# Attention row maxima from the scores' own operands, with a separate small stack of scaled keys

## What is computed

```
h = patches(x) @ W.T + b                                  # 32 images, 256 tokens, 256 wide
n = layernorm(h)
q, k, v = n@wq (16 heads of 16), n@wk, n@wv (4 heads of 16 each); rotary embedding on q and k
scores = q.k / 4, causal;  attn = softmax(scores);  h = h + (attn @ v) @ wo
h = h + ffn(layernorm(h))                                 # fake-quantised gate, up and down weights
```

## Time and profile before

| | us |
|---|---|
| median of 3 runs (826.69 to 829.05) | 828.56 |
| the profiled execution: its time | 829.71 |
| its span, first to last instruction | 828.0 |
| busy: PE / DVE / ACT / POOL | 706.0 / 648.1 / 580.7 / 569.2 |
| PE busy between 90 and 460 us, of 370 | 345.3 |

### The profile page before, as it was taken

The page is one execution under the profiler, slowest core; times in us unless marked ns, Lnnn a source line. Parts: engine busy times, 40 slices in busy tenths (PEclk is TensorE's granted clock), DMA queues, the critical chain, the costliest instruction groups (busy, mean ns, idle before and its releaser), DMA issues. The chain is left out here.

```text
span 828.0 us, 20605 instructions
## 1 busy us (share of the span) xinstructions
PE 706.0 (85%) x6706; PEld 372.8 (45%) x6706; DVE 648.1 (78%) x1048; ACT 580.7 (70%) x908; POOL 569.2 (69%) x561
## 2 busy tenths in 40 slices
PE   3577989898999999999999999999876459997894
PEld 2343545454555455545545555445322223332663
DVE  5955788788878888888888887887654359999894
ACT  3345777777788787778877778877555258886783
POOL 1355778787887888888788888786644148884363
PEclk9699999999999999999999999999868669999798
DMA  8235667666566655566666556654443123221499
GB/s 277 58 77 115 117 122 140 137 121 118 131 143 133 143 142 130 117 137 141 133 150 141 119 124 143 137 137 86 88 74 69 53 38 51 51 43 21 70 175 162
DMA packets 237190, 94.46 MB, mean 114 GB/s; under 512 B 214240, under 2 KB 232416, under 8 KB 237152
## 3 DMA queue, kind: packets, MB, share of 16 engines
q1 hardware_dynamic: 228704, 85.59, 47.7%
q0 software_dynamic: 8448, 8.39, 7.0%
HBM read 24.74 MB, written 16.78 MB: 50 GB/s over the span
## 5 line engine op out<-in xcount | busy, mean ns | idle before, releaser
L1200 DVE TENSOR_REDUCE act_all<-pair 128x4 f16<-128x1024 f32 (+1 forms) x192 | 235.1, 1225 | 30.7 <-PE pair L535 29.9
L826 ACT ACTIVATE ffn<-pair 128x768 f32<-128x768 f32 x128 | 103.2, 806 | 76.7 <-PE pair L552 76.7
L975 POOL TENSOR_SCALAR_AFFINE_SELECT act_all<-act_all 128x512 f32<-128x512 f32 x128 | 104.8, 829 | 68.7 <-ACT act_all L826 68.7
L975 POOL TENSOR_SCALAR_AFFINE_SELECT ffn<-ffn 128x512 f32<-128x512 f32 x128 | 92.8, 726 | 65.6 <-ACT ffn L826 65.6
L482 PE MATMUL pair<-act_all 128*128 128x256 f16 (+1 forms) x960 | 116.8, 275 | 17.7 <-DVE act_all L1247 15.4
L826 ACT ACTIVATE act_all<-pair 128x768 f32<-128x768 f32 x128 | 103.6, 809 | 34.2 <-PE pair L552 34.0
L482 PEld LDWEIGHTS pair<-act_all 128*128 128x128 f16 (+1 forms) x960 | 90.2, 98 | 35.8 <-issue 19.5
L1014 POOL TENSOR_TENSOR act_all<-act_all 128x1280 f16<-128x1280 f32 x31 | 81.3, 2622 | 18.7 <-ACT act_all L781 18.7
L550 PE MATMUL pair<-act_all 64*128 64x256 f16 x512 | 73.4, 283 | 11.5 <-ACT ffn L826 4.3
L496 PE MATMUL pair<-act_all 128*128 128x384 f16 x384 | 76.4, 337 | 0.1
L1186 DVE TENSOR_TENSOR act_all<-act_all 128x512 f16<-128x512 f32 x32 | 27.1, 847 | 58.1 <-ACT act_all L819 58.1
(11 more groups left out here) (133 smaller groups left out, 1492.3 us busy)
## 6 DMA issues: line engine op xcount, KB each, us to landing
act_all<-x_t SPq DMA_DIRECT2D x32, 640.0 KB, 4.2
out<-act_all SPq DMA_DIRECT2D x32, 256.0 KB, 2.6
out<-ffn POOLq DMA_DIRECT2D x16, 512.0 KB, 6.8
act_all<-act_all SPq DMA_TRANSPOSE x192, 2.8
act_all<-w_down SPq DMA_DIRECT2D x1, 704.0 KB, 8.8
act_all<-w_emb SPq DMA_DIRECT2D x1, 640.0 KB, 3.9
ffn<-w_gate SPq DMA_DIRECT2D x1, 640.0 KB, 7.1
ffn<-w_up SPq DMA_DIRECT2D x1, 640.0 KB, 8.0
```

The source lines that it names most:

```text
L826: act.activation(probs[i // 4][:, o:o + 2, 0:3, :].rearrange("p h k s -> p h (k s)"), pair[1][:, :].rearrange("p (h c) -> p h c", h=2)[:, ...
L975: pool.affine_select(out=p, in_=p, pattern=[[0, 4], [1, P]], compare_op=ALU.is_ge, fill=0.0, base=0, channel_multiplier=-1).then_inc(maske ...
L1200: dve.tensor_reduce(to, pair[2][:, :].rearrange("p (k g t) -> p k g t", k=2, g=n_), AX.X, ALU.max).then_inc(unit_reduced, 1)
```

## The change

- `max_stack`, `max_op` and `high` are gone. The queries of the units now come from the stack itself: two DMAs transpose its 16 query heads, one for each half of the tokens, 8 blocks each, into `max_q`.
- The keys of the units come from a new `key_stack` (64 columns a head, scaled by 1/64, only the columns opposite to the queries' high part filled), copied by ScalarE at the start of `fill_stack` and transposed into `max_k` by one DMA of 4 blocks. The block masks move to free columns of the stacks and of `key_stack`.
- SyncE's `turn_max` becomes `turn_max_first` (keys, queries of the first half) and `turn_max_second` (queries of the second half). The first waits for `key_ready`, `stack_filled` and `low_ready` of its image.
- The units' products use 64 rows by 128 columns of TensorE, and so do the triangles, with a wider identity `eye_wide`. Count and width of these matmuls stay the same.

```diff
-MAX_SCALE = 1.0 / 8.0
+MAX_SCALE = 1.0 / 64.0
...
-        max_stack = part(TB * QK * 32, FP16).rearrange("p (b h k) -> p b h k", b=TB, h=QK)
-        max_op = part(5 * TOKENS, FP16).rearrange("p (b g t) -> p b g t", b=TB, g=5)
+        key_stack = part(TB * KV * 64, FP16).rearrange("p (b h k) -> p b h k", b=TB, h=KV)
+        max_q = part(8 * TOKENS, FP16).rearrange("p (b g t) -> p b g t", b=TB, g=8)
+        max_k = [ffn[:, 4608 + 256 * k:4864 + 256 * k].bitcast(FP16).rearrange("p (b g t) -> p b g t", b=TB, g=2)
+                 for k in range(2)]
...
-            def turn_max(n):
-
-                sp.wait_ge(high_ready, n + 1)
+            def turn_queries(n, tb, turned):
+
+                sp.dma_start_transpose(max_q[:, tb], stacks[n % 2][:, tb, 0:HEADS, :].rearrange("p h k -> p (h k)")
+                                       ).then_inc(turned[n % 2], 16)
+
+            def turn_max_first(n):
+
+                sp.wait_ge(key_ready, n + 1)
+                sp.wait_ge(stack_filled, n + 1)
+                sp.wait_ge(low_ready, n + 1)
+                if n > 0:
+                    sp.wait_ge(unit_scored, (n - 1) * PAIRS_U + 2)
+                sp.dma_start_transpose(max_k[n % 2].rearrange("p b g t -> p (b g) t"),
+                                       key_stack.rearrange("p b h k -> p (b h k)")).then_inc(
+                                           max_first_turned[n % 2], 16)
+                turn_queries(n, 0, max_first_turned)
+
+            def turn_max_second(n):
+
                 if n > 0:
                     sp.wait_ge(unit_scored, n * PAIRS_U)
-                sp.dma_start_transpose(max_op.rearrange("p b g t -> p (b g) t"),
-                                       max_stack.rearrange("p b h k -> p (b h k)")).then_inc(max_turned[n % 2], 16)
+                turn_queries(n, 1, max_second_turned)
...
                 if (x + 2).exists():
-                    turn_max(x.n + 2)
+                    turn_max_first(x.n + 2)
+                    turn_max_second(x.n + 2)
                 if (x + 1).exists():
                     turn_stack(x.n + 1)
...
                 if p == 0:
-                    pe.wait_ge(max_turned[y.parity], y.half * 16 + 16)
+                    pe.wait_ge(max_first_turned[y.parity], y.half * 32 + 32)
+                if p == 2:
+                    pe.wait_ge(max_second_turned[y.parity], y.half * 16 + 16)
...
                     for g in range(GROUPS):
-                        for j in range(2):
-                            kv = 2 * p + j
-                            rows = slice(32 * kv, 32 * kv + 32)
-                            pe.matmul(max_bank[j][:, g * P:(g + 1) * P], max_op[rows, 0, g, :],
-                                      max_op[rows, 0, 4, :], start=(g == 0), stop=False, skip_group_check=True)
+                        for rows, b in zip(halves, max_bank):
+                            pe.matmul(b[:, g * P:(g + 1) * P], max_q[rows, 0, 2 * g + p, :], keys[rows, 0, p, :],
+                                      start=(g == 0), stop=False, skip_group_check=True)
...
-                        mm = pe.matmul(on_diagonal, eye_b[t, t],
-                                       tri_b[t, t].rearrange("p (a t) -> p a t", a=1).to_broadcast([64, n_, 64]),
+                        at_ = 64 * ((t + j) % 2)
+                        mm = pe.matmul(on_diagonal, eye_wide[rows, at_:at_ + P],
+                                       tri_b[rows, rows].rearrange("p (a t) -> p a t", a=1).to_broadcast([64, n_, 64]),
...
-            def high(x):
-
-                z = x + 2
-                act.wait_ge(qk_ready, z.n + 1)
-                wait(act, max_turned[z.parity - 1], (z + -1).half * 16 + 16)
-                act.activation(max_stack[:, :, :, 0:16], qk[:, :, :, :], ACT.Copy, scale=MAX_SCALE).then_inc(
-                    high_ready, 1)
-
             def fill_stack(x):
...
+                wait(act, max_first_turned[z.parity - 1], (z + -1).half * 32 + 32)
+                act.activation(key_stack[:, :, :, 16:32], qk[:, :, HEADS:QK, :], ACT.Copy, scale=MAX_SCALE).then_inc(
+                    key_ready, 1)
                 act.activation(stack[:, :, :, 16:32], qk[:, :, :, :], ACT.Copy)
```

More of the change, by code:

```diff
@@ L140, in vit_layer @@
         eye_k = sb("eye_k", [P, P], F32)
-        eye_b = sb("eye_b", [P, P], BF16)
+        eye_wide = sb("eye_wide", [P, P + 64], BF16)
+        eye_b = eye_wide[:, 0:P]
         ffn = sb("ffn", [P, 5120], F32)
@@ L517, in unit_pair @@
                 else:
                     for g in range(2):
[L520 to L525, removed]
@@ L527, in unit_pair @@
-                halves = (slice(0, 64), slice(64, 128)) if p % 2 == 0 else (slice(64, 128), slice(0, 64))
-                for j in range(2):
-                    for t in halves:
+                        for rows, b in zip(halves, max_bank):
+                            pe.matmul(b[:, g * TOKENS:(g + 1) * TOKENS].rearrange("p (b t) -> p b t", b=TB),
+                                      max_q[rows, 1, 2 * (2 * (p // 2 - 1) + g) + p % 2, :], keys[rows, :, p % 2, :],
+                                      start=(g == 0), stop=False, skip_group_check=True)
@@ L530, in unit_pair @@
+                for t in range(2):
+                    for j, rows in enumerate(halves):
+                        block_ = slice(64 * t, 64 * t + 64)
                         if p < 2:
-                            on_diagonal = max_bank[j][t, :].rearrange("p (g t) -> p g t", g=GROUPS)[:, :, t]
+                            on_diagonal = max_bank[j].rearrange("p (g t) -> p g t", g=GROUPS)[:, :, block_]
                         else:
-                            on_diagonal = max_bank[j][t, :].rearrange("p (g b t) -> p g b t", g=2, b=TB)[:, :, 1, t]
+                            on_diagonal = max_bank[j].rearrange("p (g b t) -> p g b t", g=2, b=TB)[:, :, 1, block_]
@@ L1002, in add_rotated @@
                 z = x + 2
-                wait(pool, high_ready, z.n)
+                wait(pool, key_ready, z.n)
                 wait(pool, stack_filled, z.n)
@@ L1124, in _ @@
                 dve.memset(stacks[k][:, :, HEADS:QK, 48:49], -M_UNIT)
-            link(dve.memset(max_stack.rearrange("p b h k -> p (b h k)"), 0.0))
+            link(dve.memset(key_stack.rearrange("p b h k -> p (b h k)"), 0.0))
             for block_ in range(TOKENS // 64):
-                at_ = max_stack[64 * (block_ % 2):64 * (block_ % 2) + 64, block_ // 2]
+                rows, tb = slice(64 * (block_ % 2), 64 * (block_ % 2) + 64), block_ // 2
                 if block_ < 3:
-                    dve.memset(at_[:, 0:HEADS, 16 + 5 * block_:21 + 5 * block_], -FAR)
+                    for k in range(2):
+                        dve.memset(stacks[k][rows, tb, 0:HEADS, 49 + 5 * block_:54 + 5 * block_], -FAR)
                 if block_ > 0:
-                    dve.memset(at_[:, HEADS:QK, 16:16 + 5 * block_], FAR)
+                    dve.memset(key_stack[rows, tb, :, 49:49 + 5 * block_], FAR)
             for k in range(2):
```

11 lines of the change are left out of this document (6 added, 5 removed).

## The result

| | before | after |
|---|---|---|
| median, us | 827.74 (4 runs) | 1026.53 (4 runs, 1025.9 to 1029.67) |
| ratio, 95% interval | | 1.2408 (1.2375 to 1.2442) |
| profiled execution, us | 829.71 | 1025.9 |
| span, us | 828.0 | 1024.1 |

The changed kernel takes 24% longer; 1030 us were predicted.

The account below looks back on a forecast made before the run. The prediction took TensorE's instruction stream to bound the kernel before. After it, a ring of 24.0 us plus 0.8 for the clock, 24.8 a step, adds 194.7 over 30 steps, and the start 7.7, to 829.7: 1030 us, range 985 to 1080.

Parts of the forecast that it names:

- The ring: Loop s0, s5, exp 5, `fill_stack`, `low`, SyncE's transposes, next s0: delay paid every step, 24.0 us before any clock loss.
- the delay is paid once: Rival: several images under way, so the delay comes once and VectorE's waits eat the switch gain; 837 us, chance 0.03.
- E to u0: From the end of `low` of the next image to its first unit's products on TensorE: 4.6 us.
- E to s0: From the end of the next image's `low`, through SyncE's transposes, to the current image's first scores: 8.3 us.
- s0 to s5: TensorE from score pair 0 to score pair 5 of an image: 12.0 us, less 0.7 for switches.
- s5 to E: From score pair 5 through exp 5, the keys' copy and `fill_stack` to the end of `low`: 4.4 us.
- The clock: TensorE's granted clock may halve after the gap before u0: 0.8 us a step, making 24.8.
- The start: First image's u0 and s0 come later, less 0.7 for copy and switches: +7.7 us once.
- The switches: TensorE's tile-shape switches drop from 28 to 16 a step, 0.10 to 0.12 us each, 1.3 us of its stream.
- Rival 1: TensorE's stream gets shorter and the later transposes hide: faster, some 793 us, chance 0.03.
- Rival 3: Only u0 delays the ring, the stack's transposes not holding up s0: step 22.3 us, 955 us in all, chance 0.06.

Follow-up runs that it names:

- experiment 1: Kernel before, with only its transpose for the maxima also waiting for `stack_filled` and `low_ready` of its image: 996.45 us, ratio 1.2061.
- experiment 6: Changed kernel with `fill_stack` ahead of exp 5, GpSimd's x_low behind mask 6, and filler matmuls in TensorE's gaps before u0 and s0: 945.35 us, ratio 1.144.
- Experiment 5: Changed kernel with `fill_stack` ahead of exp 5 on ScalarE and GpSimd's x_low moved behind mask 6: 990.72 us, ratio 1.2001.
- Experiment 2: Changed kernel with the stack's four transposes ahead of the three for the maxima in SyncE's queue: 1053.7 us, ratio 1.2752.
- experiment 8: Kernel before with all units in 64-row tiles from the old separate stack, 12 blocks in one early DMA, no wait for `low`: 824.48 us, ratio 0.9976.
- Experiment 10: Kernel before with 64-row units from an early separate stack, its transpose split into two of 6 blocks, copy behind exp 4: 817.52 us, ratio 0.9891.
- Experiment 3: Changed kernel with the stack's transposes first in SyncE's queue and 24 filler matmuls in TensorE's gap before u0: 1005.9 us, ratio 1.2173.
- experiment 7: Kernel before with the triangles alone in tiles of 64 rows by 128 columns: 833.28 us, ratio 1.0085.
- experiment 4: Changed kernel with `fill_stack` ahead of exp 5 on ScalarE: 1022.67 us, ratio 1.2363.

## Why the prediction was right, point by point

- **The ring** was the step that carried the forecast, and it is shown: experiment 1 sets it up in the kernel before with two waits, and experiment 6, with one link shorter and the clock held, gets the expected step (21.7 for 21.8 us). Experiment 5, the same link without the filler, missed its 970 by 21 us, since the clock fell. That the shapes or the number of DMAs cost most of the time is excluded by experiment 1, that the delay is paid once by the steps of 24.65 us. The 30 us between experiment 1 (996.45) and the changed kernel were not taken apart: the two more DMAs in front of the stack's belong to them.
- **Its terms**, predicted and measured: E to u0 4.6 and 4.8 (the queries land after 3.3 us, not 3.1); E to s0 8.3 and 8.47; s0 to s5 11.3 and 11.13, so that 0.9 us of switches came back where 0.7 were taken; s5 to E 4.4 and 4.69, the difference because `low` ran partly beside x_low of GpSimd and took 1.17 for 0.82 us. In sum 24.0 and 24.3. The 0.71 us that the sum takes for the second half of `low` are no fixed length either: it took 0.28 us in experiment 5, where it ended before the mask beside it. And "`high` had made its copy at 315.12" names the start of that copy; it ended at 315.85, which no term of the sum uses.
- **The clock** was the over-sized term, 0.8 us a step predicted, half of it in front of s0. It falls in the gap, as said, but it holds s0 back in no step: u0, s7 and project 0 end at 421.26, just before the stack's transposes let s0 go, and s0 waits for its DMA in all of them, 0.24 us at the least. What it costs lies behind s0 and differs from step to step. In the step from 417.87 it was back within the window 421 to 422, some 3.4 us after work began, and cost next to nothing; in the one from 491.70 it was back only behind 499, and s0 to s5 took 1.9 us more. In 18 of the 31 steps the first two matmuls of s0 took 0.39 or 0.40 us, so they ran at half clock. The mean of 24.65 leaves 0.35 us over the sum of 24.3 for it and for every other unevenness. It is dearer in experiments 1, 2 and 5.
- **The start** +7.7 and +8.4. The sum came out at 1032 and 1025.9: the clock's 0.45 us too much and the terms' 0.3 too little nearly cancel, and 2.4 us came back at the end. That the forecast is within 0.4% owes something to luck; that it is on the right side of the rivals doesn't.
- **The switches**: 0.10 to 0.12 us each before; behind them 0.06 us where the shape stays.
- **Rival 1** (the stream is the only bound) was wrong in more than the new wait: experiment 8 takes the wait away and still saves all 12 switches, and gains nothing that can be measured. The prediction read TensorE as the bound of the kernel before, since it was busy 93%. Once its stream was shorter, u0, s0, u2 and the output projection waited 0.25 to 0.37 us each for DMAs and reductions, so those paths had nearly the same length (0.15 us of wait at u0 in the earlier trace rows were the hint). Experiment 10 shortens the one to u0 and gets 1.1%.
- **Rival 3** gave 22.3 us a step for the case that the stack's transposes don't hold up s0. Experiment 2 is that case, and it gave over 25: the rival left out that they then hold up the keys' transpose, and that the slow clock then holds s0 back. Experiment 3 takes the clock out and has 23.8, of which 5.86 from E to u0 in place of the rival's 4.6: there the queue is the missed term.

## What to carry to other kernels

Before a load is moved to operands that another step writes, look up when that step ends against when the load was issued: here the old copy was ready 4.9 us earlier (315.12 + 0.73 against 320.75) than the data it was replaced by, and the load was issued at 316.65. Then follow the first instruction that gets late until the path comes back to itself; if it does, the delay is paid in every step, and its length is a sum of rows that can be added before anything is run. In a pipeline with several paths of nearly one length, time taken off the busiest engine (0.2 us a step in experiment 7, some 1.3 by estimate in experiment 8) can give nothing until the others are shortened as well.

## What the runs showed of the hardware that was not expected

- **VectorE beside GpSimd.** A subtraction of 128x512 to half precision took 0.67 us where it began ahead of GpSimd's instruction (experiment 5), 0.82 to 1.17 when partly beside GpSimd's work, and 2.79 when it began 0.4 us behind the start of a subtraction of 2.62 us on GpSimd; a scalar operation on 2 elements a lane took 0.57 us in place of 0.15 beside a mask. Moving GpSimd's instruction away took it back to 0.67 us, and the kernel from 1022.67 to 990.72 us. In the rows the subtraction on VectorE ends the same time behind GpSimd's, whenever it began: 414.50 behind 413.95 in experiment 4, 412.44 behind 411.90 in the changed kernel, 0.55 and 0.54 us. The second subtraction of `low`, of 128x128, took 0.28 us in experiment 5, and 0.71 when it ended at 413.08, 0.14 behind the mask (411.85 + 1.09); the scalar operation of experiment 7 ends at 310.52, 0.03 behind the mask. Each ends behind GpSimd by its own length less 0.12 to 0.14 us. So it looks as if VectorE's instruction doesn't run slower but stands until GpSimd's ends. The other way round it looks alike: in experiment 5 a mask began at 415.74, 0.14 us behind the first half of `low`, took 1.24 us in place of the 0.63 of the mask before it, and ended at 416.98, 0.50 behind the end of `low`. The Trainium skill, SBUF — State Buffer, Who interferes with whom, states it so: a VectorE instruction with two inputs in SBUF, and a scalar operation in one of the two-port modes, need a port that GpSimd uses, and whichever is issued first keeps it for its whole instruction while the other is blocked. These ends agree with it; the kinds of instruction were not tried one by one. The prediction took 0.82 and 0.71 us for the two halves of `low` and did not ask what would lie beside them.
- **Work that is thrown away pays.** Filler in TensorE's gaps held the granted clock at 1.00 and took 48 us (experiment 3) and 45 us (experiment 6) off. Both kernels stay slower than the kernel before.
- **A gap of 3.05 us** in front of u0 left the clock up for u0 and the start of project 0, and it fell while project 0 ran (experiment 5); a gap of 4.38 and of 5.64 us had it down when work began again.
